# A four-layer gated transformer on one core: window-attention softmax sums and centring on TensorE, and a new order of work in the first turn

## The reference

```python
k_win = k[:, :, idx].reshape(B, H, hd, T, W)      # idx: 16 shifted positions
v_win = v[:, :, idx].reshape(B, H, hd, T, W)
dots = jnp.einsum('bhdt,bhdtw->bhtw', qh, k_win) * scale
attn = jax.nn.softmax(dots, axis=-1)              # over the window of 16
out = jnp.einsum('bhtw,bhdtw->bhdt', attn, v_win)
```

## Time and profile before

| | |
|---|---|
| Times of the runs | 2133.06, 2130.57, 2121.48 us (median 2130.57) |
| The profiled execution | 2118.36 us, its span 2116.6 us |
| Mean granted clock of TensorE in it | 0.927 |
| PE busy | 1850.4 us (87%) |
| PEld busy | 1038.7 us (49%) |
| DVE busy | 1648.8 us (78%) |
| ACT busy | 583.1 us (28%) |
| POOL busy | 655.1 us (31%) |

### The profile page before, as it was taken

The page is one execution under the profiler, slowest core; times in us unless marked ns, Lnnn a source line. Parts: engine busy times, 40 slices in busy tenths (PEclk is TensorE's granted clock), DMA queues, the critical chain, the costliest instruction groups (busy, mean ns, idle before and its releaser), DMA issues. The chain is left out here.

```text
span 2116.6 us, 37275 instructions
## 1 busy us (share of the span) xinstructions
PE 1850.4 (87%) x14832; PEld 1038.7 (49%) x14832; DVE 1648.8 (78%) x2940; ACT 583.1 (28%) x1331; POOL 655.1 (31%) x786
## 2 busy tenths in 40 slices
PE   8687879888798887988874799999999999999987
PEld 6333455435554355533542355555555555555543
DVE  4489776996669966699655688888888888888895
ACT  3321233212322123222234122222222222222344
POOL 3410223002330023300222543434344444444463
PEclk8899989998799987999877899999999999999998
DMA  8737204362043610446005211111111112111011
GB/s 238 209 122 212 77 2 137 109 191 65 2 141 116 184 60 2 141 120 180 1 1 174 80 51 51 51 51 50 51 51 46 51 35 66 26 46 31 26 41 51
DMA packets 141771, 176.48 MB, mean 83 GB/s; under 512 B 46752, under 2 KB 81728, under 8 KB 141472
## 3 DMA queue, kind: packets, MB, share of 16 engines
q1 hardware_dynamic: 139584, 172.88, 27.6%
q10 hardware_dynamic: 2016, 1.22, 0.3%
HBM read 131.98 MB, written 42.08 MB: 82 GB/s over the span
## 5 line engine op out<-in xcount | busy, mean ns | idle before, releaser
L1266 POOL TENSOR_TENSOR early_vare<-early_mv,w_eps 128x1 f32<-128x1 f32 x96 | 29.7, 309 | 750.2 <-DVE early_mv L1349 741.4
L2404 POOL TENSOR_TENSOR la_q<-la_straight,la_rot 128x512 f32<-128x512 f32 x128 | 163.0, 1274 | 163.7 <-DVE la_rot L2474 163.7
L434 PE MATMUL la_ps<-w_xTh,w_wqh 128*128 128x512 bf16 x512 | 196.2, 383 | 14.4 <-POOLq L116 8.0
L832 PE MATMUL early_ps<-early_products,w_heads 128*32 128x512 f32 x1024 | 140.1, 672 | 63.4 <-DVE early_products L1502 35.9
L435 PE MATMUL la_ps<-w_xTl,w_wqh 128*128 128x512 bf16 x512 | 195.0, 381 | 0.0
L436 PE MATMUL la_ps<-w_xTh,w_wql 128*128 128x512 bf16 x512 | 194.6, 380 | 0.0
L434 PE MATMUL la_ps<-w_woh,la_oTh 128*128 128x512 bf16 x512 | 194.0, 379 | 0.3 <-issue 0.3
L435 PE MATMUL la_ps<-w_wol,la_oTh 128*128 128x512 bf16 x512 | 194.0, 379 | 0.0
L436 PE MATMUL la_ps<-w_woh,la_oTl 128*128 128x512 bf16 x512 | 194.0, 379 | 0.0
L2417 POOL TENSOR_TENSOR la_p<-la_s,la_rec 128x256 f32<-128x256 f32 x128 | 89.9, 703 | 273.3 <-DVE la_rec L2495 273.3
L2336 ACT ACTIVATE la_oTh<-la_ps 128x256 bf16<-128x256 f32 x256 | 84.0, 380 | 293.5 <-PE la_ps L2219 293.5
(11 more groups left out here) (352 smaller groups left out, 4609.4 us busy)
## 6 DMA issues: line engine op xcount, KB each, us to landing
early_vR<-scr_v SPq DMA_DIRECT2D x128, 257.0 KB, 5.2
early_wkv<-wkv SPq DMA_DIRECT2D x32, 512.0 KB, 4.5
la_v<-v SPq DMA_DIRECT2D x64, 256.0 KB, 4.0
k<-early_ctxt SPq DMA_DIRECT2D x32, 256.0 KB, 3.9
v<-early_ctxt SPq DMA_DIRECT2D x64, 128.0 KB, 3.0
scr_p<-early_weights SPq DMA_DIRECT2D x16, 512.0 KB, 2.6
early_pR<-scr_p SPq DMA_DIRECT2D x32, 256.0 KB, 3.5
w_raw_q<-in_Wq SPq DMA_DIRECT2D x8, 1024.0 KB, 7.4
```

The costliest lines, as they stand in the source:

```text
L434: pe.matmul(out, lh[c], rh[c], start=(first and c == 0), stop=False)
L832: last = pe.matmul(out[32 * g:32 * g + 32, :], w["heads"][:, HEADS * (1 - odd):HEADS * (1 - odd) + 32], src(2 * g + odd), start=(opens and ...
L2404: rope_sum.send(pool.tensor_tensor(dst, straight[:, slot, :], rot[:, slot, :], ALU.add))
```

## The change

In layer 1's attention the largest value stays a VectorE reduction, now negated. TensorE adds it onto the scores in PSUM, with the identity as stationary and the maxima broadcast over the window as moving operand (`centre`). ScalarE exponentiates from PSUM, in two halves, and writes `ee` with the window outermost (`ee_by_window`). TensorE sums the sixteen window positions by identity matmuls of 64 columns into a new PSUM step `wsum` (`sum_weights`). VectorE takes the reciprocal from there, and multiplies in the order of memory. The subtraction and the sum on VectorE are gone. On every engine the steps of the attention have a new order.

In turn 0, SP loads bq, bk and Wk first and Wq in two halves; r and s are computed before M, and c after it. The high parts of R1, W1 and the rest are made between ScalarE's `aT_high` copies; the signs of W2 are made after the scores of layer 0. `hsT_copy` stands ahead of the splits 6 and 7 on ScalarE, POOL has `rstd_of` ahead of splits it stood behind, and SP has another order of keeping splits, writing values and loading them. The positions are loaded and computed at another place, and the last tile's values are loaded in two parts around the write of its weights (not shown).

```diff
...
-        sp.dma_start(self.wq[:, :, :], io["L0_Wq"].rearrange("(c p) n -> p c n", p=P)).then_inc(self.loaded, 16)
-        sp.dma_start(self.wk[:, :, :], io["L0_Wk"].rearrange("(c p) n -> p c n", p=P)).then_inc(self.loaded, 16)
-        sp.dma_start(self.bq[:, :], io["L0_bq"]).then_inc(self.loaded, 16)
-        sp.dma_start(self.bk[:, :], io["L0_bk"]).then_inc(self.loaded, 16)
+        sp.dma_start(self.bq[:, :], io["L0_bq"]).then_inc(self.wk_loaded, 16)
+        sp.dma_start(self.bk[:, :], io["L0_bk"]).then_inc(self.wk_loaded, 16)
+        sp.dma_start(self.wk[:, :, :], io["L0_Wk"].rearrange("(c p) n -> p c n", p=P)).then_inc(self.wk_loaded, 16)
+        for h in range(2):
+            cols = slice(2 * h * P, 2 * (h + 1) * P)
+            sp.dma_start(self.wq[:, :, cols], io["L0_Wq"].rearrange("(c p) n -> p c n", p=P)[:, :, cols])\
+              .then_inc(self.wq_loaded[h], 16)
         sp.dma_start(self.gates_raw[:, :], io["gates"].partition_broadcast(P)).then_inc(self.gates_loaded, 16)
 
     def load_raw(self, sp, *names):
...
         wq, wk, bq, bk = self.wq, self.wk, self.bq, self.bk
-        pe.wait_ge(self.loaded, 4 * 16)
-        for m in range(C):
...
+        banks.wait_free(pe, 0, "s")
+        for c in range(C):
+            last = pe.matmul(banks.bank("s")[:, 0:1], bq[:, c:c + 1].to_broadcast([P, P]), bk[:, c:c + 1],
+                             start=(c == 0), stop=(c == C - 1))
+        banks.fill(last, "s")
+        for m in range(C):
...
+                                 start=(c == 0), stop=(c == C - 1))
+            banks.fill(last, "M", m)
         banks.wait_free(pe, 0, "c")
         for m in range(C):
             for c in range(C):
                 last = pe.matmul(banks.bank("c")[:, m:m + 1], wq[:, c, m * P:(m + 1) * P], bk[:, c:c + 1],
                                  start=(c == 0), stop=(c == C - 1))
         banks.fill(last, "c")
...
     for f, layer in ((0, 1), (1, 3)):
         if f == 1:
             for j in range(QUAD):
+                if j == 3:
+                    plan.append((("wsum", 0), 0))
                 plan += [(("q1", j), 0), (("k1", j), 1)]
+            plan += [(("wsum", j), 0) for j in range(1, QUAD)]
             for j in range(QUAD):
                 plan += [(("dot1", j, 0), 4), (("dot1", j, 1), 5)]
                 plan += [(("sum1", j), 2), (("out1", j), 3)]
...
+            ee_by_window = ee[:, :, :].rearrange("p t w -> p (t w)").rearrange("p (w t) -> p w t", t=TP)
             y1 = xn
...
                     if j == 1:
-                        for k in range(2):
-                            load_values(sp, turn, k)
+                        if turn == 0:
+                            first_keys_values(3)
+                        else:
+                            for k in range(2):
+                                load_values(sp, turn, k)
                 if turn == 0:
-                    first_keys_values(4, 5, 6, 7)
+                    first_keys_values(4, 5)
+                    load_values(sp, turn, 0)
                     for g in range(2):
+                        first_keys_values(KV - 2 + g)
                         prep.wait_kv_kept(sp, KV - 2 + g)
                         load_kv_weights(turn, g)
+                    load_values(sp, turn, 1)
                 for f in range(3):
                     keep_kv(turn, f)
                 weights_by_shift(turn, 0)
...
+                banks.wait_filled(sp, turn, "sum1", 1)
+                load_values(sp, turn, 3, range(CH // 2))
+                write_weights(turn, 3)
+                load_values(sp, turn, 3, range(CH // 2, CH))
+                read_weights(turn, 3)
                 for f in range(12, 2 * KV):
...
                                    "dot1", j, h)
+
+                def centre(j):
+                    for h in range(2):
+                        mx1_ready.wait(pe, turn, 2 * j + h)
+                        at = slice(h * (TP // 2), (h + 1) * (TP // 2))
+                        centred.send(pe.matmul(banks.bank("dot1", j, h).rearrange("p (t w) -> p t w", w=WIN), ident,
+                                               mx1[:, at].unsqueeze(2).to_broadcast([P, TP // 2, WIN]),
+                                               start=False, stop=True, skip_group_check=True))
+
+                def sum_weights(j):
+                    banks.wait_free(pe, turn, "wsum", j)
+                    for h in range(2):
+                        banks.wait_drained(pe, turn, "dot1", j, h)
+                    for k in range(WIN):
+                        last = pe.matmul(banks.bank("wsum", j)[:, 0:TP], ident, ee_by_window[:, k, :],
+                                         start=(k == 0), stop=(k == WIN - 1))
+                    banks.fill(last, "wsum", j)
 
                 def sum_window(j):
...
                 queries_keys(1)
-                last_keys_values(0)
+                last_keys_values(0, 1)
                 sum_depth(0)
                 queries_keys(2)
-                last_keys_values(1, 2)
+                centre(0)
+                last_keys_values(2)
+                sum_weights(0)
                 sum_depth(1)
                 queries_keys(3)
-                last_keys_values(3, 4, 5)
+                centre(1)
+                last_keys_values(3, 4)
+                sum_weights(1)
                 sum_depth(2)
-                last_keys_values(6, 7)
+                last_keys_values(5, 6)
                 sum_window(0)
                 out_proj(0)
-                last_keys_values(8, 9)
+                centre(2)
+                last_keys_values(7, 8)
+                sum_weights(2)
                 sum_depth(3)
-                last_keys_values(10, 11)
+                last_keys_values(9, 10)
+                centre(3)
+                last_keys_values(11)
+                sum_weights(3)
                 sum_window(1)
...
             def exponentials1(turn, j):
-                banks.wait_drained(act, turn, "dot1", j, 0)
-                banks.wait_drained(act, turn, "dot1", j, 1)
-                exp1_ready.send(act.activation(ee[:, :, :], ee[:, :, :], ACT.Exp, scale=float(CH) ** -0.5))
+                for h in range(2):
+                    at = slice(h * (TP // 2), (h + 1) * (TP // 2))
+                    if h == 0 and j >= 1:
+                        p1_ready.wait(act, turn, j - 1)
+                    centred.wait(act, turn, 2 * j + h)
+                    banks.drain(act.activation(ee_by_window[:, :, at],
+                                               banks.bank("dot1", j, h).rearrange("p (t w) -> p w t", w=WIN),
+                                               ACT.Exp, scale=float(CH) ** -0.5), "dot1", j, h)
 
             def out_copy(turn, j):
...
                     aT_high.send(act.activation(aTh[:, j, :, :], aT[:, j % 2, :, :], ACT.Copy))
+                    if turn == 0 and j < 3:
+                        prep.high(act, *(("R1",), ("W1",), ("Wqd", "Wkv", "R3"))[j])
                 if turn == 0:
...
                 route_exp(turn, 0, e0, R0)
-                if turn == 0:
-                    prep.split_kv_high(act, 6)
                 hsT_copy(turn, 0)
                 if turn == 0:
-                    prep.split_kv_high(act, 7)
+                    prep.split_kv_high(act, 6, 7)
                 queries_keys(turn, 0)
                 queries_keys(turn, 1)
-                last_keys_values(turn, 0)
+                last_keys_values(turn, 0, 1)
+                queries_keys(turn, 2)
                 exponentials1(turn, 0)
-                queries_keys(turn, 2)
-                last_keys_values(turn, 1, 2)
+                last_keys_values(turn, 2)
                 queries_keys(turn, 3)
-                last_keys_values(turn, 3)
                 exponentials1(turn, 1)
-                last_keys_values(turn, 4, 5, 6, 7)
+                last_keys_values(turn, 3, 4, 5, 6)
                 out_copy(turn, 0)
+                y1_copy(turn, 0)
                 exponentials1(turn, 2)
-                y1_copy(turn, 0)
-                last_keys_values(turn, 8, 9, 10, 11)
+                last_keys_values(turn, 7, 8, 9, 10)
+                exponentials1(turn, 3)
+                last_keys_values(turn, 11)
                 out_copy(turn, 1)
-                exponentials1(turn, 3)
                 y1_copy(turn, 1)
...
                 if turn == 0:
-                    prep.split_kv_low(pool, 0, 1, 2, 3)
+                    prep.split_kv_low(pool, 0, 1, 2)
+                rstd_of(turn, 1)
+                if turn == 0:
+                    prep.split_kv_low(pool, 3)
                     pool.wait_ge(prep.biased, 1)
-                rstd_of(turn, 1)
                 add_bias(turn, 0, 1)
                 if turn == 0:
-                    prep.split_kv_low(pool, 4, 5, 6, 7)
+                    prep.split_kv_low(pool, 4, 5)
                 rstd_of(turn, 2)
+                if turn == 0:
+                    prep.split_kv_low(pool, 6, 7)
                 rstd_of(turn, 3)
...
```

(29 more changed lines are left out.)

66 lines of the change are left out of this document (30 added, 36 removed).

## The result

The changed kernel takes 2132.15 us by median (2125.97 to 2140.95), the kernel before, run beside it, 2122.24: ratio 1.0041, 95% interval 1.0024 to 1.0058, +9.9 us. That is slower, and less than the 0.5% that the forecast called no change; the forecast was 2144.6. The kernel before now has more runs: its median is 8.3 us under the 2130.57 from which the forecast started.

A forecast was written before the change was run, and what follows sets the result against it. VectorE was taken to bound layer 1's attention, TensorE close behind. Turn 0 at -1 us and turns 1 to 3 at +15 gave +14 on a median of 2130.57: 2144.6 us, range 2122 to 2168.

The forecast's parts named there:

- What bounds: Layer 1's attention: VectorE bounds, busy 102 us a turn; TensorE is close behind with 20.6 us idle to give.
- VectorE's loss: Layer 1's attention: subtractions, sums and strided reading go, 13.2 us less per turn, leaving VectorE about 89 us.
- TensorE's gain: Layer 1's attention: centring 6.9 us and four sums 13.9 us, together 20.8 us more per turn.
- The stages of turns 1 to 3: Layer 1's attention in turns 1 to 3: TensorE sets the end, +5 us a turn, +15 in all.
- Turn 0: Turn 0: earlier start mostly lost to late K/V product 0; -1 us, between -11 and +4.
- The rival that turn 0 pays in full: Turn 0: first K/V weights back when wanted, gain 15 less 3.7 us, total 2130 us; chance 0.20.
- The clock: TensorE in layer 1's attention: fewer waits bring back some granted clock; one slow stretch kept, one lost.
- the rival that the sums slow it: TensorE's sums: half of sixteen run at 6.8 us instead of 3.5, 26 us more, 2171 us; chance 0.14.
- The sum: Whole kernel: -1 us in turn 0 and +15 in turns 1 to 3, +14 us, 2144.6 us by median.
- TensorE taking the end over: Layer 1's attention: the main forecast, TensorE sets the stage's end, 2144.6 us; chance 0.54.
- the forecast's own part of it: Whole kernel: the main forecast's own range, 2133 to 2160 us, inside the full range of 2122 to 2168.
- The rival that TensorE had room: TensorE's sums: below 1.8 us each, VectorE stays the bound and the change pays, 2063 us; chance 0.12.

The follow-up runs named there:

- e1: The changed kernel with centring and sums given back to VectorE, all new orders kept; 2115.09 us, 0.9972 of the kernel before.
- e10: The kernel before with turn 0's new order only, layer 1's steps as before; 2112.70 us, ratio 0.9945.
- e3: The changed kernel with only the centring back on VectorE, sums staying on TensorE; 2100.46 us, 0.9898 of the kernel before.
- e17: e10 with VectorE's maxima and differences of tile 3 moved ahead of tile 1's value product; 2105.28 us, 0.9923 of the kernel before.
- e4: The changed kernel with half the windows left out of every sum, not a complete kernel; 2093.46 us, 0.9868 of the kernel before.
- e2: The changed kernel with only the sums back on VectorE, centring staying on TensorE; 2115.77 us, 0.9978 of the kernel before.
- e8: The changed kernel with sums on GpSimd, tile 2 and 3 loads released earlier, tile 3's weights written first; 2129.08 us, 1.0044 of the kernel before.
- e13: The changed kernel with tile 3's value loads issued by ScalarE's queue; 2135.70 us, 1.0057 of the kernel before.
- e14: e3 with tile 3's value loads issued by ScalarE's queue; 2117.63 us, 0.9978 of the kernel before.

## Why the prediction was right or wrong

**The step that failed.** The forecast gave the whole +5 us a stage of turns 1 to 3 to TensorE's added work and took the new order of layer 1's steps at nothing, without a reason. e1 has both new orders and none of the added work, and its stages are 5.6, 2.7 and 2.3 us longer than before, 10.6 of the changed kernel's 14.0. Turn 0's new order alone (e10) gives 1.5 of these. The added work on top of e1 put on 3.3 us (-0.5, +1.6 and +2.2), not 15. What the forecast left out is a chain of DMAs: VectorE waits 7 to 9 us a turn for the weights of tiles 2 and 3 in e1, 2 before. That the sum came near is in part luck. How the 14.0 us divide depends on which change is made first, and no run has the added work in the old order, so that share stays open. The other miss is the base: the forecast started at 2130.57, so its 2144.6 asked for 22.4 us over the later median of 2122.24, of which 9.9 came.

**What bounds.** Right as far as it went: TensorE close behind VectorE, and room for one of the two moves only. It left out the third party: the DMAs for tiles 2 and 3, whose wait of 1.9 us in before was the sign of a chain that VectorE's work nearly covered.

**VectorE's loss.** 13.2 us forecast; 101.9 to 89.6 is 12.3. The division is 1.225 us (1.21 forecast).

**TensorE's gain.** A sum takes 3.6 us (399.08 to 402.69; forecast 3.5), a centring pair 1.7 us (394.78 to 396.49; 1.72), 14.4 + 6.8 us a turn for 13.9 + 6.9. The neighbours L300 and L306 with one column were the right ones: the f32 weight load sets the pace at 64 columns too (PEld is busy 3.54 of a sum's 3.61 us).

**The stages of turns 1 to 3.** +5 each; measured +5.1, +4.3, +4.6. The size is right and the account in part: e3 to after, the centring alone at full TensorE, is +4.0 to +5.5 for 6.8 us of work, so TensorE does set the end there. But its waits in turn 1 are 7.4 us, 2.9 of them before the last projection, behind the DMA. And of the 2.3 to 5.6 us a stage in e1, e17 accounts for 2.1 to 3.3 by 2.7 us of VectorE's steps moved out from under the DMA chain. With TensorE late as well the two don't add: from e1 to the changed kernel the stages change by -0.5, +1.6 and +2.2 us.

**Turn 0.** -1 us; measured +0.5. Its steps hold: first projection at 102.2 (forecast 104), K/V product 0 at 115.21 behind a DMA (115.7), the 14.3 us wait at 6.1, VectorE's first product 13.1 us sooner (15). The reason given was too narrow. The forecast blamed the late K/V product 0; e10, with that product as late, gains 10.9 us. What eats the gain is the rest of the change: +7.4 us from the new order of layer 1 (e10 to e1) and +3.9 from the added work of both kinds (e1 to after). Of the 7.4, some 3 stand already at tile 1's first key product on VectorE (123.81 in e10, 126.86 in e1), where K/V product 1 has come ahead of tile 0's depth sum. The rival that turn 0 pays in full had the right size, 15 less 3.7 us, for a kernel without the rest of the edit, but not its mechanism: it wanted product 0 on time.

**The clock.** The granted clock in the stages of turns 1 to 3 rose to 0.98 to 1.00, so the part of the forecast that it comes back held, and the rival that the sums slow it fell: their 14.8 us a turn stand at full rate, in turn 0 too, though that stage has 0.94 (0.97 before). Outside of the stages the kernel lost 2.2 us net, which the forecast didn't look at: +4.7 in the first stretch, whose clock fell from 0.90 to 0.84, and -2.5 in the other two.

**The sum.** +14 us forecast, +15.7 in the profiled executions, +9.9 by the medians. TensorE taking the end over held in part, as said above. Of the 12.4 us between 2144.6 and 2132.15, 8.3 are the base, a median of three runs, and 4.1 the change itself: the profiled executions differ by 1.7 us more than the forecast, and lie 5.8 us further apart than their medians. The time lies in the range, 0.85 us under the forecast's own part of it; slower by over 0.5%, given the most, didn't come, within 0.5% did.

**The rival that TensorE had room** (2063 us) fell by the price of a sum, 3.6 us against 1.8, and e4 showed 1.8 to be the point. By the Trainium skill (Perfetto Trace Analysis, Identifying the Most-Contended Engine) weight-load busy time is the measure of headroom; in the changed kernel it is 53% of the stage (59.9 of 113.1 us, turn 2) while VectorE waits 11.8 us for TensorE's sums. The waits, not that share, told it here.

## What to carry over

Price a gift of work to a second engine against that engine's idle time as it is spent, wait by wait: one of two moves may fit where both don't, and the half that fits (e3, with the same new orders) was worth 1.0% where the whole cost 0.4%. Before moving a step of the bounding engine ahead of something, look whether a DMA chain covered it where it stood. In a queue that runs in order, any wait for a slow producer (here the K/V stores) holds every transfer behind it: put what is ready first.

## What the runs showed of the hardware

An f32 matmul with a 128x128 stationary and 64 columns runs at 0.113 us per instruction (3.6 us for 32), as with one column (0.109): the weight load sets the pace, and PEld is busy 3.54 of the 3.61 us. Reading PSUM with a stride of 16 elements costs nothing on ScalarE (0.597 us for 512 elements, the time of a plain copy of 512) nor on VectorE (0.691 us for the subtraction of 512, in order in the kernel before and strided in e3). VectorE's reading of SBUF with a stride does cost: 1.90 against 1.225 us for a product of 1024 at a stride of 16 elements, 1.99 against 1.21 for a sum of 1024 at a stride of 64 (e2). GpSimd's additions of 256 columns took 0.73 us by themselves and up to 4.79 beside VectorE's key products of 4.42 us (e8). The write of tile 3's weights, 512 KB beside eight loads of 257 KB, landed in 5.5 to 6.4 us in the kernel before and the changed kernel, and in 9.3 to 10.5 in e13 and e14, where ScalarE's queue issued the loads; the median of all such writes in the kernel before is 2.6.
